# A decoder layer on one core: own orders for the first two and the last two steps of the recurrence pipeline

## The reference

```python
x = x + rwkv(layernorm(x))            # recurrence, 8 heads of 64
x = x + cross(layernorm(x), ctx, mask)  # attention over ctx, 16 heads of 32
x = x + ffn(layernorm(x))             # two ternary linear layers, 512 -> 2048 -> 512

# rwkv
xx  = shifted(x) - x
a   = tanh((x + xx * maa_x) @ w1).reshape(B, T, 5, 32)
m   = einsum('btfd,fdc->fbtc', a, w2)
xw, xk, xv, xr, xg = (x + xx * (maa_j + m_j) for j in "wkvrg")
r, k, v = xr @ W_r.T, xk @ W_k.T, xv @ W_v.T
g   = silu(xg @ W_g.T)
w   = time_decay + tanh(xw @ wd1) @ wd2
S_t = exp(-exp(w_t)) * S_{t-1} + k_t v_t^T
y_t = r_t (S_{t-1} + u * k_t v_t^T)
out = groupnorm(y) * g @ W_o.T

# ffn: each weight matrix is rounded to -1, 0, 1 times mean(|w|)
```

## Time and profile before

| | before |
|---|---|
| median of 3 runs | 876.15 us |
| the profiled execution | 875.0 us |
| its span | 873.2 us |
| PE busy | 827.3 us (95%) |
| DVE busy | 738.1 us (85%) |
| ACT busy | 505.0 us (58%) |
| POOL busy | 139.1 us (16%) |
| mean granted clock of PE | 0.98 |

### The profile page before, as it was taken

One profiled execution on the slowest core, in us unless ns is written; L12 is line 12 of the kernel. 1 busy time (PEld: TensorE's weight loads), 2 busy tenths in 40 slices (PEclk: granted clock), 3 DMA queues, 4 the chain that ended last, 5 costly groups with the idle time before them and its releaser, 6 DMA issues.

```text
span 873.2 us, 23820 instructions
## 1 busy us (share of the span) xinstructions
PE 827.3 (95%) x10117; PEld 666.5 (76%) x10134; DVE 738.1 (85%) x1206; ACT 505.0 (58%) x728; POOL 139.1 (16%) x197
## 2 busy tenths in 40 slices
PE   7898999999999999999889999999999978999997
PEld 6798988888898888889777788888888845444453
DVE  5987989899898989986575689889888979999995
ACT  5566372846546374643535436435444457999995
POOL 1001020100102010100102000000000123676441
PEclk9899999999999999999879999999999989999999
DMA  8330112030211202023140340430232120242311
GB/s 256 126 110 19 44 34 90 15 110 15 69 44 50 75 14 86 15 86 108 65 170 2 146 162 8 146 144 29 115 144 97 39 98 25 87 143 98 109 67 55
DMA packets 36553, 72.41 MB, mean 83 GB/s; under 512 B 6081, under 2 KB 6977, under 8 KB 35433
## 3 DMA queue, kind: packets, MB, share of 16 engines
q1 hardware_dynamic: 35912, 68.93, 23.9%
q0 software_dynamic: 544, 2.10, 0.6%
HBM read 58.39 MB, written 12.58 MB: 81 GB/s over the span
## 4 chain that ended last, share of the span: by engine, by line
PE 72%; DVE 16%; issue 5%; POOL 4%; ACT 1%; DMA 1%; DVEq 0%; POOLq 0%; SPq 0%; ACTq 0%
PE P L62 11%; PE P L63 9%; PE P L64 9%; PE S L750 6%; PE S L2290 5%; PE P L2276 4%; POOL sm L378 3%; DVE xf L1026 3%; DVE E L1862 2%; PE S L636 2%; PE S L1723 2%; PE S L62 2%; PE S L63 2%; PE S L64 2%; PE S L1710 2%
## 5 line engine op out<-in xcount | busy, mean ns | idle before, releaser
L378 POOL TENSOR_TENSOR sm<-sm,mhalf 128x16 f32<-128x16 f32 x8 | 30.6, 3828 | 303.7 <-DVE sm L1121 303.7
L2290 PE MATMUL S<-wq,hqT 128*128 128x512 bf16 x255 | 59.9, 380 | 2.6 <-ACT hqT L2214 2.2
L750 PE MATMUL S<-R,K 64*64 64x32 f32 x3072 | 57.2, 223 | 2.8 <-DVE K L1072 1.7
L750 PEld LDWEIGHTS S<-R,K 64*64 64x64 f32 x3072 | 51.5, 137 | 10.4 <-issue 4.7
L2276 PE MATMUL P<-wq,xqT 128*128 128x512 bf16 x240 | 56.1, 387 | 2.3 <-ACT xqT L2192 1.2
L1862 DVE TENSOR_SCALAR E<-S,upper 128x2048 f32<-128x2048 f32 x16 | 37.6, 2349 | 24.2 <-PE S L1710 24.0
L1536 ACT ACTIVATE E<-E 128x2048 f32<-128x2048 f32 x16 | 30.6, 1913 | 45.3 <-DVE E L1862 45.3
L1868 DVE RECIPROCAL rec<-S 128x512 f32<-128x512 f32 x16 | 53.6, 3350 | 1.8 <-PE S L1725 1.8
L1026 DVE TENSOR_TENSOR xf<-P,xx 128x1024 f32<-128x1024 f32 x40 | 48.7, 1218 | 7.3 <-PE P L657 7.2
L1033 DVE TENSOR_TENSOR xf<-xf,xnT 128x1024 f32<-128x1024 f32 x40 | 49.1, 1227 | 1.1
L2276 PEld LDWEIGHTS P<-wq,xqT 128*128 128x128 bf16 x256 | 24.7, 100 | 29.3 <-issue 2.7
(11 more groups left out here) (300 smaller groups left out, 2701.0 us busy)
## 6 DMA issues: line engine op xcount, KB each, us to landing
wch<-in_wff SPq DMA_DIRECT2D x32, 256.0 KB, 3.1
cwch<-in_wff SPq DMA_DIRECT2D x8, 1024.0 KB, 7.0
xt<-in_x SPq DMA_DIRECT2D x8, 512.0 KB, 4.5
y<-in_x SPq DMA_DIRECT2D x8, 512.0 KB, 3.6
out<-y SPq DMA_DIRECT2D x8, 512.0 KB, 3.3
cxt<-out SPq DMA_DIRECT2D x8, 512.0 KB, 4.1
ct<-in_ctx SPq DMA_DIRECT2D x8, 512.0 KB, 5.1
cxr<-out SPq DMA_DIRECT2D x8, 512.0 KB, 7.0
```

The lines of the kernel that those rows point to most:

```text
L378: pool.tensor_tensor(sm[:, 2, :], sm[:, 1, :], mhalf[:, 0:2 * H], ALU.pow).then_inc(y_rstd, 1)
L750: mm = pe.matmul(ps[half_rows(side), par, b, k, :], K[head_rows(par), r % 2, at:at + HALF], right_tokens(par, g, side, i), start=True, sto ...
L2290: mm = pe.matmul(O[:, :], hqT[b % 2][:, k, :], w2q[:, k, :], start=k == 0, stop=k == NF - 1)
```

## The change

The conditions in `step` go; the first two steps that compute (s = 1 and 2), the closing step and the last step get their own functions on ACT, PE and DVE, with their own order. The six steps between keep theirs, but for three things: `stack_first` copies four rows (not two) of `stack` and `stack_middle` the next two before the narrow tanh, `token_shift` waits for each of its four inputs by itself, and in the first full step (q = 1) the transpose of x comes first.

In the first step PE waits for each of the three pieces of `w2` by itself, has fewer fillers, and begins the k projection of pair 0 there instead of in the second step.

```diff
+        def first_step():                       # PE
+            keep_busy(X2, 8)
+            turn_in(0)
+            keep_busy(X2, 12)
...
+            token_shift(0)
+            narrow(0, None)
+            keep_busy(L, 3)
+            mix(0, 0, X0)
+            keep_busy(L, 6)
+            pe.wait_ge(mix_ready, 1)
+            mix(0, 1, X0)
...
+            keep_busy(X2, 20)
+            pe.wait_ge(wsplit_lo, 1)
+            pe.wait_ge(lo_ready, 1)
+            pe.wait_ge(mix_ready, 3)
+            channel_major("k", X0, 0)
+            mix(0, 3, X1)
```

```diff
+        def second_step():                      # DVE
+            xf_sum(0, 4)
+            lo(0, 3)
+            shift(1)
+            maa_x(1)
+            split_weight("r")
+            lo(0, 4)
+            lower_stack(1, 0, 2)
+            low_v(0)
+            low_v(1)
+            mix(1, 0)
```

The sums of |w| have new places on ACT in the first steps. Before, parts 2 and 3 of pair 0's piece stood at the end of the first step, and those of pair 1's at the end of the second; now they are moved one step on, and the first full step (q = 1) makes six sums instead of four:

```diff
             if f:
                 hi(p, 3)
-                abs_sum(p, 2)
+                abs_sum(p, 1 if q == 1 else 2)
             if n is not None:
...
             if f:
+                if q == 1:
+                    abs_sum(p, 2)
                 abs_sum(p, 3)
```

PE's new last step has a chunk behind every level from level 0 on, and one chunk of the second pair at its end:

```diff
+        def last_step(r):                       # PE
+            turn_bonus(r)
+            level(r, 0)
+            pe.wait_ge(g_ready, PAIRS)
+            x["q_chunk"](0, 0)
+            level(r, 1)
...
+            level(r, 6)
+            x["k_chunk"](0, 2)
+            first_values(r)
+            x["k_chunk"](0, 3)
+            second_values(r)
+            x["sum_weights"]()
+            x["project_bv"]()
+            x["v_rows"](0, 0)
+            turn_y(r)
+            x["turn_x"](1)
+            x["v_rows"](0, 1)
+            project_o(r)
+            x["q_chunk"](1, 0)
```

More of the change, by code:

```diff
@@ new lines, in copy_v, with tanh_g, normalize @@
+        def copy_v(q):
+            act.wait_ge(v_done, q + 1)
+            if q > 0:
+                act.wait_ge(y_done, q)
+            act.activation(V[:, :, :].rearrange("p b c -> p (b c)"), X0[:, :], ACT.Copy).then_inc(v_ready, 1)
+        def tanh_g(q):
+            act.wait_ge(g_done, q + 1)
+            if q > 0:
+                act.wait_ge(z_gated, q)
+            act.activation(S[:, :, :].rearrange("p k t -> p (k t)"), X0[:, :], ACT.Tanh, scale=0.5).then_inc(g_tanh, 1)
+        def normalize(n):
+            act.wait_ge(shifted, n + 1)
+            for b in range(2):
+                act.activation(xt[:, b, :], xt[:, b, :], ACT.Identity, bias=shf[:, b:b + 1], scale=rsf[:, b:b + 1]).then_inc(xn_ready, 1)
@@ new lines, in affine_z, with high_z @@
+        def affine_z(r):
+            act.wait_ge(y_turned, r + 1)
+            if r == 0:
+                act.wait_ge(setup, 5)
+            else:
+                act.wait_ge(zl_ready, r)
+            for k in range(NC):
+                act.activation(z[:, k, :], X2[:, 2 * T * k:2 * T * (k + 1)], ACT.Identity,
+                               bias=beta[:, k:k + 1], scale=gamma[:, k:k + 1]).then_inc(z_affine, 1)
+        def high_z(r):
+            act.wait_ge(z_gated, r + 1)
+            act.wait_ge(r_done, min(r + 2, PAIRS))
+            if r > 0:
+                act.wait_ge(o_done, r)
+            act.activation(half["r"][0][:, :, :], z, ACT.Copy).then_inc(zh_ready, 1)
@@ L931, in step @@
-            if s_:
-                token_major("v", half["v"], X0, 1).then_inc(v_done, 1)
-            if f and not t_:
-                mix_3(p, q)
-            if t_:
-                pe.wait_ge(y_scaled, r + 1)
-                for k in range(NC):
-                    for b in range(2):
-                        mm = turn(X2[:, (2 * k + b) * T:(2 * k + b + 1) * T], y[:, b, P * k:P * k + P])
-                mm.then_inc(y_turned, 1)
-            if last:
-                x["v_rows"](0, 1)
-                x["turn_x"](1)
@@ new lines, in first_step @@
+        def first_step():
+            shift(0)
+            maa_x(0)
+            low_w2(0)
+            lower_stack(0, 0, 2)
+            mix(0, 0)
+            xf_sum(0, 0)
+            mix(0, 1)
+            low_w2(1)
+            lower_stack(0, 2, 4)
+            lower_g(0)
+            xf_sum(0, 1)
+            mix(0, 2)
+            split_weight("k")
+            lo(0, 1)
+            norm(1)
+            low_w2(2)
+            xf_sum(0, 2)
+            mix(0, 3)
+            norm_shift(1)
+            xf_sum(0, 3)
+            lo(0, 2)
+            mix(0, 4)
@@ new lines, in last_step @@
+        def last_step(r):
+            for i in range(5):
+                level(r, i)
+            place_bonus(r)
+            level(r, 5)
+            x["norm"](1)
+            x["split_weight"]("v")
+            x["norm_shift"](1)
+            x["split_weight"]("o")
+            y_stats(r)
+            x["bounds"]()
+            x["sum_bias"]()
+            y_scale(r)
+            z_gate(r)
+            x["low_x"](1)
+            lower_z(r)
+            x["low_ctx"](1)
+            add_rows(r)
+            x["lower_bias"]()
```

1017 lines of the change are left out of this document (562 added, 455 removed).

## The result

The changed kernel takes **861.22 us** (median of 4 runs, 860.52 to 862.53), the kernel before on the same chip 875.69 us (4 runs, 874.18 to 876.9): a ratio of 0.9837, with a 95% interval of 0.9817 to 0.9857. The forecast was 859.5 us, with a range of 854 to 866. The profiled execution took 862.53 us against 875.0, with a span of 860.7 us.

The account below looks back on a forecast made before the run. Full steps leave PE 0.64 us idle; time is lost to DVE's idling while filling and PE's idling and low clock in closing and last steps. 7.7 - 3.6 - 0.9 + 5.1 + 7.7 = 16.0 us off 875.0: 859.5 us, range 854 to 866.

Parts of the forecast that it names:

- signs of being wrong: Clock at 0.50 in the last step, a full step 1 us longer or shorter, or first full step's stretch starting after 84 us.
- the first scaling near 80.4 us: End of the filling: DVE's first scaling of R would come near 80.4 us, against 88.09 before.
- the idle time of 2.3 us in the last step: Last step: PE would wait about 2.3 us ahead of y's transpose.
- Filling: While the pipeline fills: DVE loses less time waiting, so its first scaling of R comes 7.7 us earlier.
- The third sum: End of first full step: a third sum of |w| waits for its load, so the next step begins 3.6 us later.
- The rival on the clock: Clock falls in the new last step or again while filling: 863 us, both together 866; 20% chance.
- Full steps: Six steps: one more `stack` row copied by ACT ahead of the narrow tanh costs 0.15 us each, 0.9 us.
- Closing step: Squares no longer wait for the split of `Xq`, y's transpose finds no gap, clock stays: 5.1 us gained.
- Last step: Chunks between levels fill PE's waits and the y chain shortens: 7.7 us gained up to the cross attention's first scores.
- bound of 9.5: Last step: upper bound of the gain, if DVE and PE lose nothing between levels and POOL's power takes 2.90 us.
- the wait at 488.06 us: Ahead of the scores in the last step: a wait of 1.31 us, to be covered by the chunk of pair 1.
- move along: Behind the first scores: cross attention and feed-forward layer keep their order and only shift in time, 0 us.

Follow-up runs that it names:

- experiment 7: Changed kernel with one sum of |w| moved behind the exponentials (first full step) and the rows of ones behind the first shift_r: 853.38 us, ratio 0.9747.
- experiment 3: Changed kernel with DVE's rows of ones behind the first shift_r instead of ahead of it: 859.38 us, ratio 0.9812.
- experiment 2: Changed kernel with 11 fillers on PE ahead of level 1 of the recurrence in the second full step: 862.47 us, ratio 0.9853.
- Experiment 5: Changed kernel with ACT's split of Xq in the closing step ahead of the squares of y, as in the kernel before: 864.13 us, ratio 0.9865.
- experiment 4: Changed kernel with DVE's low half of Wo (Xo) behind the sum of squares in the last step, as before: 863.52 us, ratio 0.9853.
- experiment 6: Changed kernel with PE's chunks of the first q and k projections in the last step two levels later, as before: 865.63 us, ratio 0.9895.

## Why the prediction was right, point by point

**The total** was right, 1.7 us from the median, and all three stretches that were to give time gave it. That it came so near is in part luck. The sum was 3.4 us too favourable in the profile (-16.0 against -12.6), from errors of both signs, and one of the prediction's own signs of being wrong came: a full step 7.1 us longer, where 1 us was to be too much. Of its signs of being right, the closing step and the clock from 410 to 450 us came; the first scaling near 80.4 us and the idle time of 2.3 us in the last step did not.

**Filling, -7.7 forecast, -5.9 measured.** The walk of DVE's list was right in its length from `xx` on: 69.70 us, and 68.97 where PE was quick (experiment 7), against the 69.1 of the forecast. It assumed the four inputs of the token shift at 14.2 us as before. They came 1.2 us late, and mix 0 started at 19.41 us, not 16.9. The rows of ones, which the sum moved "ahead of 14.2 us, where DVE idles", stand beside POOL's power. That is the step that failed: DVE's time was free there, POOL's was not (0.6 us), and the moment at which PE gains speed gave or took 1.6 us at the first scaling (experiment 3). With both in its favour experiment 7 reached 80.03 us, against the 80.4 forecast. What the new orders on PE and DVE give apart from each other was not tested; no run puts one of them back.

**The third sum, +3.6 forecast, +7.1 measured.** The wait was right to 0.1 us (experiment 2: 53.65 against 50.07). The mis-sized part is its consequence on PE: the forecast carried it to the start of the next step as a plain delay and did not ask whether PE would stand still long enough to lose the clock. The rival on the clock named the last step and the filling, and a price of 2.5 to 3.5 us, which is what it cost, at a third place. The forecast's bounds of 0 to 4.0 us did not hold the 7.1.

**Full steps, +0.9 forecast, -0.5 measured.** No cost of the later narrow tanh shows; no run takes it apart. The difference is within what one step varies: between the y powers, two steps of before take 50.75 and 50.92 us and one of after 50.99, the others 50.0 to 50.2.

**Closing step, -5.1 forecast, -5.2 measured.** Squares at 410.8, no gap ahead of y's transpose, full clock. Experiment 5 gives the order of the split 2.4 us by its stretch; the rest was not taken apart.

**Last step, -7.7 forecast, -9.1 measured.** Up to the second `values` it was -4.9 instead of -5.7. From there to y's transpose 7.0 us instead of 9.0: the forecast kept POOL's 4.87 us of before instead of asking what ran beside it, though the earlier trace rows had 2.90 for the same instruction (its bound of 9.5 allowed for it). With it went the gap of 2.3 us and the rival that hung on it; experiment 4 brings both back. The chunks behind levels 0 and 1 are the larger part: without them the step is 7.2 us longer (experiment 6), though part of that is a stop whose cause is open. By the rule of the Trainium skill ("TensorE: Matmul & The Clock Gate", Part 4: PE-mode transpose) that transposes don't count as PE work in the same way, a gap with transposes behind it should be the dangerous kind. The runs don't decide it: the clock fell in experiment 4, behind 2.05 us and with two transposes, and stayed in 5, behind 2.54 us and one.

**Behind the scores, 0 forecast, +1.0.** From the first scores to POOL's next small power it takes 7.04 us (483.27) instead of 5.77 (495.45). The trace shows why. DVE there waits 1.17 us for the load of the next pair's rows, `cxt<-out`, in the kernel after and 0.88 to 1.18 us in all eight experiments; before it did not wait. The load is issued behind the store of the last rows y, at 476.58 us, 0.35 us behind the scores' start; before it was issued at 488.46, 1.22 us ahead of them. The chunk of pair 1, which now fills PE's wait for y, brought the scores nearer to y but not the load, which hangs on y. So the 1.3 us that the forecast took off for the wait at 488.06 came at the scores and were lost again at the load; "move along" was wrong by that much.

## What to carry to other kernels

A load that is issued only when the piece before it has been used has a fixed distance to its use (here some 3.2 us): give every such use its own idle slot in the engine's list, and don't put two behind one another at a step's end. When a wait is moved, follow it to PE and price it twice, once as a delay and once as a gap, behind which the clock may halve (here for 3 to 10 us); then ask which engine sets the pace there, since the fall cost 3.5 us at 137 us and nothing at 24. A time saved ahead of a load counts only if the load starts earlier too. A duration on POOL is read together with the DVE instruction that is running when it starts.

## What the runs showed of the hardware

- The fall of PE's clock behind a gap is no fixed price, and no length of gap decided it here. It fell to 0.50 behind gaps of 1.78, 1.98, 2.05 and, in five profiles out of five, the 2.35 to 2.99 us of the third sum, and in experiment 6 amid gaps of 0.51, 0.53 and 1.25 us. It stayed at 1.00 behind the 2.54 us of experiment 5, behind 1.96 to 1.98 us at the same place of the program as the 1.98 (seven profiles), and behind 2.18 to 2.19 us in the filling in seven profiles out of nine. Behind the third sum it stayed low for 3 to 4 us (powers 54.07 us apart in experiment 6, 54.76 in 3) or 10 us (57.17 after, 57.41 in 4, 57.22 in 5). So two versions that differ by one small gap can't be told apart to better than about 3 us by one profile.
- POOL's power of 128x16 took 2.90, 3.81 or 4.87 us and that of 128x2 between 0.70 and 2.67 us. It ended 2.75 or 0.55 to 0.59 us behind the end of the DVE instruction that was running when it started; DVE's own instructions showed no delay.
- In the first 15 us the same fillers and transposes ran at half speed up to a moment between about 9 and 14 us that differed between profiles, with a granted clock of 1.00 in every window. It moved the end of the filling by 1.6 us.
